# Statistics of the last sixteen tiles moved behind the first half's expert choice, with the dense work relisted and the scatters' named waits removed

## The reference, cut to what matters

```python
xn = layernorm(x)
q, k, v = xr @ Wq.T, xr @ Wk.T, xr @ Wv.T            # per head of 8
attn = softmax((q * k).sum(-1) / sqrt(128), axis=0)[..., None] * v.sum(axis=1)
scores = softmax(xn @ gate_w + gate_b)               # 16 experts
top_vals, top_idx = top_k(scores, 2)
y = sum over the two experts: weight * ((silu(xn @ w1 + b1) * (xn @ w3 + b3)) @ w2 + b2)
z = silu(xn @ sw1 + sb1) * (xn @ sw3 + sb3) @ sw2 + sb2      # 352 inner columns
out = x + attn + y + z
```

## Time and profile before

| | us |
|---|---|
| median of 3 runs | 283.98 (282.92 to 284.85) |
| span of the profiled execution | 275.7 |
| median less that span | 8.3 |
| first of the 64 scatters issued | 29.3 |
| last dense up-projection begins | 112.9 |
| last of the 64 scatters issued | 132.5 |
| first result scatter issued | 138.3 |

### The profile page before, as it was taken

How to read it: one execution, slowest core, us unless ns; L and a number is a source line. 1 busy time by engine, 2 the same in 40 slices (tenths; PEclk the granted TensorE clock), 3 DMA queues, 4 the chain that set the end, 5 groups by cost and what they waited for, 6 DMA issues and landing times.

```text
span 275.7 us, 4667 instructions
## 1 busy us (share of the span) xinstructions
PE 217.2 (79%) x1289; PEld 174.1 (63%) x1289; DVE 155.8 (57%) x423; ACT 100.9 (37%) x220; POOL 156.0 (57%) x169
## 2 busy tenths in 40 slices
PE   8989995987909969958598876977685995986860
PEld 6655683744706736457597775877675994986730
DVE  5998838689426934722366653555441452376562
ACT  2378854032013522511344432333441443434400
POOL 7238675674754760747255654556455564655573
PEclk9999979899865999988689999999999798999995
DMA  6999997112353243111122333233222358527256
GB/s 209 350 398 288 209 210 196 54 55 92 123 162 118 85 125 89 55 34 54 36 81 81 92 84 92 73 83 84 69 82 82 89 144 223 161 74 262 76 193 228
DMA packets 28397, 36.48 MB, mean 132 GB/s; under 512 B 5123, under 2 KB 23811, under 8 KB 28019
## 3 DMA queue, kind: packets, MB, share of 16 engines
q1 hardware_dynamic: 22724, 22.87, 28.4%
q0 software_dynamic: 5104, 12.79, 15.7%
q10 hardware_dynamic: 544, 0.52, 0.5%
HBM read 21.81 MB, written 14.35 MB: 131 GB/s over the span
## 4 chain that ended last, share of the span: by engine, by line
PE 40%; another core or an unknown queue 24%; DVE 14%; issue 13%; ACT 7%; DMA 1%; DVEq 0%; ACTq 0%
PE PS L1092 6%; PE PS L1214 6%; PE PS L1069 6%; PE PS L1070 6%; PE PS L1244 4%; DVE XR L515 3%; DVE sS L819 2%; PE PS L1229 2%; ACT prod L995 2%; DVE rxl L814 2%; PE PS L1201 2%; ACT sS L1001 2%; PE PS L1038 2%; PE PS L1057 2%
## 5 line engine op out<-in xcount | busy, mean ns | idle before, releaser
L490 POOL DMA_INDIRECT ydram<-fw x79 | 77.3, 979 | 60.5 <-DVE fw L823 39.0
L481 POOL DMA_INDIRECT xslot<-XR,idx x64 | 63.4, 990 | 42.7 <-issue 18.2
L1244 PE MATMUL PS<-fw,sS 89*128 (+1 forms) x316 | 44.0, 284 | 0.0
L1244 PEld LDWEIGHTS PS<-fw,sS 89*128 89x128 f32 (+1 forms) x316 | 40.6, 200 | 0.1
L823 DVE TENSOR_TENSOR fw<-PS,fw 128x256 f32<-128x256 f32 (+1 forms) x40 | 16.8, 419 | 35.1 <-remote 17.4
L1229 PE MATMUL PS<-kc,sS 128*88 128x128 f32 x158 | 25.1, 283 | 14.3 <-DVE sS L819 9.2
L1092 PEld LDWEIGHTS PS<-sw,sS 128*128 128x128 f32 (+1 forms) x192 | 27.5, 229 | 12.5 <-issue 12.5
L1092 PE MATMUL PS<-sw,sS 128*128 128x128 f32 (+1 forms) x192 | 28.3, 315 | 8.6 <-issue 5.8
L990 ACT ACTIVATE rxh<-PS 128x256 fp32r<-128x256 f32 (+1 forms) x40 | 15.2, 381 | 54.0 <-remote 31.2
L819 DVE TENSOR_TENSOR sS<-prod,PS 128x352 f32<-128x352 f32 (+1 forms) x40 | 20.6, 514 | 24.3 <-ACT prod L995 19.8
L1214 PE MATMUL PS<-w13h,rxh 128*128 x79 | 29.9, 379 | 0.8 <-DVE rxl L814 0.8
(11 more groups left out here) (147 smaller groups left out, 318.3 us busy)
## 6 DMA issues: line engine op xcount, KB each, us to landing
fw<-xslot SPq DMA_DIRECT2D x79, 72.0 KB, 1.9
fw<-wdram SPq DMA_DIRECT2D x1, 2816.0 KB, 11.4
fw<-in_w POOLq DMA_DIRECT2D x1, 2816.0 KB
X<-in_x SPq DMA_DIRECT2D x8, 256.0 KB, 5.2
XR<-ydram SPq DMA_DIRECT2D x4, 512.0 KB, 3.7
fw<-in_w SPq DMA_DIRECT2D x1, 1536.0 KB
xnT<-ydram SPq DMA_DIRECT2D x3, 512.0 KB, 4.5
out<-X SPq DMA_DIRECT2D x5, 256.0 KB
```

The lines of the kernel that those rows point to most:

```text
L481: pool.indirect_dma_start(xslot, bass.IndirectOffsetOnAxis(ap=idx[:, k, t:t + 1], axis=0), XR[:, t, :], None).then_inc(d_sc[k][h][q], 16)
L490: pool.indirect_dma_start(ydram, bass.IndirectOffsetOnAxis(ap=RX[:, v, TOK:TOK + 1].bitcast(I32), axis=0), yb[:, v, :], None).then_inc(d_y ...
L1244: ins = pe.matmul(PS[:, DN_BANK[b], i * P:(i + 1) * P], raT[0:n, b, (2 * i + k) * P:(2 * i + k + 1) * P], w2[0:n, bass.ds(e * 2 * P + k * ...
```

## The change

- **Order of the front.** `norm(3)` goes from VectorE to GpSimd (`POOLED` is now (3,)), groups 4 and 5 go to VectorE. The statistics of groups 4 to 7, their inverses and their norms are taken out from ahead of the first half's choice and placed behind it, between dense work of groups 0 to 3. GpSimd does its norm ahead of the masking of the attention weights (`wbd`).
- **Order of the dense work.** The groups 2 and 3 now use the PSUM banks of `early` ((1, 2) and (3, 6)), transposes from group 4 on use bank 0 alone, and `down` of groups 0 to 3 bank 5. TensorE does `down(0)`, `up(2, ...)`, `down(1)` and group 3 before and between the transposes and logits of groups 4 to 7; the second half's choice on VectorE comes behind `gated_up(3, 2)`; `down(3)` stands ahead of `rank(1)` on TensorE; `gated_up(4, 0)` ahead of `index(0, 1)` on VectorE.
- **Scatters.** The three tables of named waits are gone. The first eight scatters come ahead of the accumulating DMA, all others behind it. The rest of the order is as before, and so are the waits on row numbers, weights and `second_place`.
- Helper functions take a piece (first tile, number of tiles) in place of a half; with two pieces of sixteen they do the same operations. `gate` on GpSimd is renamed `mark`. The expert loop and the tail are unchanged.

```diff
-POOLED = (4, 5)
+POOLED = (3,)
...
+G_AT = ((4, 0), (7, 0))
+UP_EARLY = ((1, 2), (3, 6))
...
+            def scatter(k, u):
...
+            pool.wait_ge(s_idx, 1)
+            pool.wait_ge(s_cw, 1)
+            scatter(0, 0)
             pool.wait_ge(d_wb, 16)
             pool.dma_start(w13, d["w13"], accum_op=ALU.add, max_dma_last_dim=NBIAS).then_inc(d_wa, 16)
...
-                            if n in PACE_UP:
-                                pool.wait_ge(s_up, PACE_UP[n])
...
+            scatter(0, 1)
+            pool.wait_ge(s_idx, 2)
+            pool.wait_ge(s_alt, 2)
+            scatter(1, 0)
+            pool.wait_ge(s_alt, 4)
+            scatter(1, 1)
+            pool.wait_ge(s_idx, 3)
+            pool.wait_ge(s_cw, 3)
+            scatter(0, 2)
+            scatter(0, 3)
+            pool.wait_ge(s_idx, 4)
+            pool.wait_ge(s_alt, 6)
+            scatter(1, 2)
+            pool.wait_ge(s_alt, 8)
+            scatter(1, 3)
```

More of the change, by code:

```diff
@@ L1069, in up @@
                 pe.matmul(PS[0:m, k, :], sw1[:, f:f + m], xv, start=True, stop=True)
-                pe.matmul(PS[0:m, 2 + k, :], sw3[:, f:f + m], xv, start=True, stop=True).then_inc(s_up, 1)
+                pe.matmul(PS[0:m, l, :], sw3[:, f:f + m], xv, start=True, stop=True).then_inc(s_up, 1)
             def early(n):
@@ L1106, in _ @@
             turn(2)
+            early(1)
             turn(3)
-            early(1)
             logits(2)
```

465 lines of the change are left out of this document (238 added, 227 removed).

## The result

| | before | changed |
|---|---|---|
| median, us | 283.45 (282.84 to 284.85, 4 runs) | 310.18 (307.31 to 310.77, 4 runs) |
| ratio | | 1.092, 95% interval 1.085 to 1.098 |
| span of the profiled execution | 275.7 | 308.7 |
| end of VectorE's last split (the front's end) | 117.0 | 149.8 |
| from there to the end of the span | 158.7 | 158.9 |

The change costs 26.7 us, where 286 had been forecast and 296 was the upper end of the range. The front carries all of it: the loop behind is as long as it was, so the assumption that a shift of the front's end goes one for one into the span held (32.8 us of front, 33.0 of span; the profiled execution of before was some 6 us shorter than its usual ones).

What follows compares the result with a forecast made beforehand. VectorE's list and completions delayed by scatter runs were taken to bound the front: 112 plus 6 gives 118 to 119 against 117.0, so span 275.7 + 1.7 = 277.4, plus 8.3 outside it, say 286 us; range 274 to 296.

Steps and rivals of the forecast that it cites:

- The +6 us for late completions: Front: TensorE's down-projections reach VectorE late during scatter runs once the named waits go; +6 us (5 to 7).
- VectorE's list without late completions: Front: VectorE's remaining work, the new chain and about 1 us of short waits end the front at 112.
- The yardstick: Front's end: the new order's 111.2 was set against the measured 117.0 of before, so 5.8 us earlier.
- the rival with prompt completions: Front: completions come promptly or the new order hides them; 5 to 8 us faster, 276 to 279; chance 0.31.
- The 8.3 us "outside the span": Whole kernel: time outside the profiled span, 8.3 us, added to the forecast span of 277.4 to give 285.7.
- 46.2 us of VectorE's work at 59.5, so 105.7.: Front: VectorE passes the second-place copy at 59.5 with 46.2 us of work left, so ends at 105.7.
- The new chain ahead of the second row numbers: Behind the second choice, VectorE waits for add_z(2), down(3), rank(1), up(4, 0), silu and gating: +5 to +6 us.
- The wait for the landing behind the accumulating DMA: VectorE at second_place(0, 1): scatters queued behind that DMA land at 59.5, a wait of 6.7 us, or 0.
- The first scatter: GpSimd: first choice at 18.8 instead of 19.5, first scatter at about 27.8 instead of 29.34; 1.5 us gained.
- Late completions: Front: scatter runs delay TensorE's completions by 3 to 7 us; down(0) and down(1) absorbed, down(2) 0 to 2, down(4) 4.
- The third rival: Front: a scatter run holds completions until GpSimd stops; front's end at 126, 293 us; chance 0.27.
- The signs: Changed profile: first scatter 27 to 28.5, landing 57 to 62, remote waits 15 to 25 us, last up-projection 114 to 117.

Runs made afterwards that it cites:

- a0: The changed kernel as it is, measured again where completions were prompt: 239.29 us, ratio 1.092 to the kernel before.
- k1: The kernel before without its named waits, nothing else changed: 218.46 us (0.999) with prompt completions; measured again with late ones, 299.25 us (1.063).
- k3: The changed kernel with the accumulating DMA moved ahead of all scatters: 241.92 us, ratio 1.108 to the kernel before.
- f5: The changed kernel with reordered tail, second choice and front, plus 20 waits put back among its scatters: 231.51 us, measured again 230.18 us.
- e5: The changed kernel with the statistics of groups 4 to 7 moved back ahead of the first choice: 239.91 us, ratio 1.096 to the kernel before.

## Why the prediction was wrong, point by point

**The +6 us for late completions (the step that failed).** The sum was 112 for VectorE's list without late completions, plus "+6 (5 to 7)" for them, 118 to 119 in all; measured was 149.8. The same kernel in a prompt group (a0) ends its front at 120.7. So in these two executions the late completions, with what follows from them, cost 149.8 - 120.7 = 29.1 us where I had 6, and the list itself came to 120.7 where I had 112: 23.1 + 8.7 = 31.8 us, the whole miss. The mechanism behind the 6 was wrong as well: I charged the down-projections alone and let VectorE's wait at 59.5 absorb the first of them. Held were the up-projections on their way to ScalarE, behind which stand the copies that TensorE waits for.

**The yardstick.** The 6 looked small because I set the new list against the 117.0 of before, "5.8 before 117.0", while 112 was worked "without late completions" and 117.0 has them: by my own rows 3.5 + 7.2 + 4.3 = 15.0 us lie ahead of it, and k1 shows 98.5, so 18.5. A like front of before would have ended at 102 by my rows, and the new order would have lost 10 us by my own sum before any completion was late; it loses 22.1. That is also why the rival with prompt completions, 276 to 279 and so 5 to 8 us faster, was no way out: there the change costs 20.9 us. The 8.3 us "outside the span" had a like fault. The profile of before was of an unusually short execution; the changed kernel has 310.52 - 308.7 = 1.8 us outside its span.

**"46.2 us of VectorE's work at 59.5, so 105.7."** The work was right, the packing was not. In a0 VectorE passes the copy at 60.99 and its last split ends at 120.65; it is busy 44.9 of these 59.7 us. The 14.7 us of idle time are 8.32 for the new chain (I had 5.5), 4.8 ahead of three gatings of the tail (2.54, 1.66 and 0.61), and short gaps; for all but the chain I had allowed "about 1 us". I had taken VectorE for the engine the front hangs on; k1 shows that in the old order it is TensorE once completions are prompt, and an order for a front without holes can't be judged by another engine's busy time. In the late group the same 45.3 us of work took 86.8.

**The new chain ahead of the second row numbers.** Held in kind and priced too low: VectorE idle 6.69 us ahead of the gating of `up(4, 0)` in the profiled execution, for the 5 to 6 forecast, and 8.32 in a0.

**The wait for the landing behind the accumulating DMA.** The mechanism and its time held where completions are prompt: VectorE waited until 60.99 (I had 59.5, and a window of 57 to 62) for 5.45 us (6.7). In the late group VectorE came at 62.97, so the data were there. k3, without a wait at this copy once the transfer stood first, fits it. The page of the Trainium skill that the prediction cited ("DMA: Bandwidth & Descriptors", Queues, rings and completion order) says that descriptors are consumed in ring order, and says it of the queues of SyncE and ScalarE; that the scatters land late on GpSimd's queue too is what the 5.45 us show.

**The first scatter.** 31.35 for 27.8, and 29.59 in a0. The norm on GpSimd took 3.31 us (3.1 forecast). I had overlooked ScalarE: `copies(3)` stands behind the evacuation of `early(1)`, so the choice starts at 22.3 (20.55 in a0), not 18.8. In f5 and f5_again, with the two exchanged, the choice still waits 2.84 and 3.77 us for the logits.

**Late completions.** I read the four late down-projections of before rightly and priced the wrong victims: `down(0)` and `down(1)` were on time in the first 15 us of the run, and the late ones were `up(3, 1)`, `up(3, 2)`, `up(5, 1)`, a projection and the slot table's matmul, by 7 to 12 us each. `up(3, 1)` came through at 61.58, 12 us before its run of scatters ended, so a stop of GpSimd is not always needed. The third rival, "a run holds completions until it stops", came nearest in kind: in k1_again a completion was held for 27.6 us until GpSimd stood. Its price, 293, was too small, since it rested on the same yardstick.

**The signs.** The last up-projection began at 142.99 (114 to 117 forecast) and the first result scatter at 168.69 (138 to 142). Ahead of the additions of the dense results there was no remote wait at all in the front, where I had 15 to 25 us, and less than 8 was to mean prompt completions. In a late group that sign pointed the wrong way: I watched the additions, and the waits stood ahead of ScalarE's gates. The loop kept its pace, as I had said.

**What each cause is worth.** In prompt groups the order alone costs 20.9 us (239.29 less 218.41). In the late group the change costs 26.7. If the order costs as much there, some 6 us are left for held completions and lost waits, though the same waits are worth 14 to 18 us in the old order there. The two do not add up. The rows give a reason, which was not tested: in the new order GpSimd stands still for 23.80 and 22.79 us waiting for VectorE, so it stops by itself where the waits would have stopped it.

**Still open.** What makes a group late: up to 30 us the profiles look alike (TensorE busy 27.75 us in before, late, and 28.10 in k1, prompt), and one late and one prompt group ran on a chip of the same number. How the order's 20.9 us divide: mends of tail, choice and front together brought 8 to 9 back (with the waits in, which alone bring nothing in a prompt group), the tail alone 2.2, and some 12 us are not accounted for; of the front's and the choice's shares there is only the sum.

## What to carry to other kernels

Before a new list is set against an old one, take out of both the waits that neither list causes; a yardstick with 15 us of them flatters every new order. Look for the engine that hardly idles in the yardstick without those waits: here TensorE with 5.0 us of 98.5, against 17.6 for VectorE, whose busy time I forecast to 3% and which gave me the wrong end all the same. And when a mend gains nothing, read which wait grew by what it gave: e5's statistics turned up in the wait for a landing, so that wait has to be moved before such a mend can show.

## What the runs showed of the hardware

- The same kernel takes 283 to 285 us or 218.5 us, with single instructions as long in both. In the late groups completions arrive 3 to 12 us late, once 27.6, while GpSimd issues indirect scatters. In two groups of six it was there, in four not at all (a share of 28% of the chain against none for k1). Of the 59.3 us by which the profiled spans of before and k1 differ (275.7 and 216.4), 40.8 fall behind the front.
- In k1_again, while completions were held, TensorE itself slowed to one matmul in 1.4 to 2.8 us without any wait in the trace, and SyncE's 16 register reads with their DMAs took 41 us in place of 13 (23 in the changed kernel). TensorE, VectorE and ScalarE went on 4 us after GpSimd's last scatter. The hold is therefore not of TensorE's completions alone, as I had read it from the profile of before.
- Named waits in GpSimd's scatters were worth 14 to 18 us of 285 in a late group and 0.0 of 218.5 in a prompt one. A measurement in one condition says nothing on the other.
